# Even heads squared and summed by ScalarE in four accumulating operations, odd heads summed by VectorE

## The reference

```python
h = _layernorm(x, axis=-1) * (1 + ca) + sa
# in the attention part, on h:
q, k, v = ...                       # projections; q and k are rotated
scores = einsum('bhtd,bhsd->bhts', q, k) * D ** (-0.5) * decay
o = einsum('bhts,bhsv->bhtv', scores, v)
mean, var = o.mean(-1), o.var(-1)   # over the 128 values of one head and token
o = (o - mean) * rsqrt(var + EPS)
o = o * gn_weight + gn_bias
o = o * silu(g)
out = einsum('btc,oc->bto', o, Wo)
```

## Time and profile before

| | |
|---|---|
| runs shown | 746.31 us median of 3 (746.22 to 746.49) |
| the profiled execution | 747.0 us, of which its span on the core is 745.2 us |
| TensorE's granted clock | 0.998 of full speed on average |
| busy over the span | TensorE 98%, its weight loads 86%, GpSimd 82%, VectorE 81%, ScalarE 64% |

### The profile page before, as it was taken

The page is one execution under the profiler, slowest core; times in us unless marked ns, Lnnn a source line. Parts: engine busy times, 40 slices in busy tenths (PEclk is TensorE's granted clock), DMA queues, the critical chain, the costliest instruction groups (busy, mean ns, idle before and its releaser), DMA issues.

```text
span 745.2 us, 29021 instructions
## 1 busy us (share of the span) xinstructions
PE 732.8 (98%) x12119; PEld 643.9 (86%) x12119; DVE 604.6 (81%) x1268; ACT 480.6 (64%) x928; POOL 607.5 (82%) x652
## 2 busy tenths in 40 slices
PE   8999999999999999999999999999999999999997
PEld 7778888888889889888888988888888888988986
DVE  4997688888888888888788888888898788787547
ACT  4666657676665666666676665766666666656665
POOL 5887779889798897988889798888979888687640
PEclk9999999999999999999999999999999999999999
DMA  6610020200202121030211303021030201001101
GB/s 251 194 32 18 15 59 15 60 18 13 83 17 77 27 65 39 10 94 17 69 27 21 87 14 88 10 80 30 11 87 17 73 17 31 17 9 31 25 15 29
DMA packets 59809, 35.15 MB, mean 47 GB/s; under 512 B 36664, under 2 KB 54432, under 8 KB 59680
## 3 DMA queue, kind: packets, MB, share of 16 engines
q1 hardware_dynamic: 58960, 32.51, 16.9%
q10 hardware_dynamic: 720, 0.80, 0.3%
HBM read 20.66 MB, written 4.25 MB: 33 GB/s over the span
## 4 chain that ended last, share of the span: by engine, by line
PE 92%; DVE 3%; POOL 2%; ACT 1%; issue 1%; DMA 1%; SPq 0%; DVEq 0%
PE ring L332 51%; PE outs L332 15%; PE O_E L332 14%; PE ring L347 8%; PE O_O L332 3%; PE ring L397 1%; DMA N<-in_w_qkT 1%; POOL gn_rstd L1466 0%; ACT normed L751 0%; POOL y L1473 0%; ACT y L815 0%; DVE N L1146 0%; DVE A L1119 0%; DVE qT L1080 0%; POOL rot_k L1456 0%
## 5 line engine op out<-in xcount | busy, mean ns | idle before, releaser
L1473 POOL TENSOR_TENSOR y<-y,gate 128x512 f32<-128x512 f32 x120 | 158.8, 1337 | 29.4 <-ACT y L815 29.4
L779 ACT ACTIVATE v<-ring 64x512 f32<-64x512 f32 x128 | 76.2, 595 | 80.7 <-PE ring L332 79.9
L332 PEld LDWEIGHTS outs<-wo_gated,y 128*128 128x128 f32 x992 | 119.8, 192 | 6.7 <-DVE y L1185 0.5
L1456 POOL TENSOR_TENSOR rot_k<-rot_k,sin_k 128x256 f32<-128x256 f32 x128 | 102.6, 822 | 26.9 <-DVE sin_k L1112 25.6
L332 PE MATMUL outs<-wo_gated,y 128*128 128x128 f32 x992 | 121.7, 275 | 0.1
L1466 POOL TENSOR_TENSOR gn_rstd<-gn_var,minus_half 128x8 f32<-128x8 f32 x64 | 105.4, 1646 | 5.0
L787 ACT ACTIVATE kT<-ring 128x512 f32<-128x512 f32 x64 | 38.4, 599 | 100.6 <-PE ring L347 100.6
L1139 DVE TENSOR_REDUCE gn_sum<-N 128x4 f32<-128x512 f32 x118 | 75.3, 679 | 26.4 <-ACT N L803 26.4
L1119 DVE TENSOR_TENSOR A<-ring,consts 128x256 f32<-128x256 f32 x128 | 48.4, 419 | 57.5 <-PE ring L332 57.5
L815 ACT ACTIVATE y<-ring,gn 128x512 f32<-128x512 f32 x126 | 91.0, 777 | 5.2 <-PE ring L347 5.2
L1450 POOL TENSOR_TENSOR qT<-qT,swapped 128x512 f32<-128x512 f32 x60 | 77.1, 1284 | 11.3 <-DVE swapped L1095 10.7
(11 more groups left out here) (198 smaller groups left out, 2119.4 us busy)
## 6 DMA issues: line engine op xcount, KB each, us to landing
k_odd<-rot_k SPq DMA_DIRECT2D x128, 64.0 KB, 2.2
row_of<-written_rows SPq DMA_DIRECT2D x12, 512.0 KB, 4.2
X<-in_x SPq DMA_DIRECT2D x16, 256.0 KB, 4.4
out<-X SPq DMA_DIRECT2D x15, 256.0 KB, 2.4
x_turned<-in_xT SPq DMA_DIRECT2D x12, 256.0 KB, 4.6
key_tables<-in_const SPq DMA_DIRECT2D x7, 256.0 KB, 5.1
rotary_q<-in_const_q SPq DMA_DIRECT2D x2, 512.0 KB, 6.1
gates<-stored_rows SPq DMA_DIRECT2D x8, 128.0 KB, 3.1
```

The source lines that it names most:

```text
L332: return e.matmul(o, lhsT, rhs, start=start, stop=stop, skip_group_check=True)
L779: done = e.activation(v[halves(half), i % 2, 1, :, :], by(PAIRS, bank_of["v", odd, i][halves(1 - half), :]), ACT.Copy)
L1456: done = e.tensor_tensor(turned[:, n, :, :], turned[:, n, :, :], sin[:, n, :, :], op)
L1473: e.tensor_tensor(y[:, n % NY, :], y[:, n % NY, :], gate[:, n % 2, :], ALU.mult).then_inc(sem["y"])
```

## The change

In all chunks the even heads now go the way that the first five went: four operations of ScalarE of 128x128, each with its sum. The odd heads are squared in one operation and summed by VectorE as before. VectorE's sum of the even heads is gone.

```diff
@@ -792,7 +792,7 @@ square(i, odd)
                 at.wait_ge("nT_psum", PAIRS * ((i - NN) // GC + 1))
-                if i < EARLY:
+                if i < EARLY or not odd:
                     at.wait_ge("gn_var", i - 1)
                     for n in range(PAIRS):
                         done = e.activation(N[:, i % NN, odd, n, :], heads_of(i)[odd][:, n, :], ACT.Square, accum_out=gn_sum[:, i % 2, odd, n:n + 1])
@@ -1339,8 +1339,6 @@ the loop of block.vector
                 for i in due(step - 1, 1, NCHUNK, 5):
-                    sum_squares(i, 0)
-                for i in due(step - 1, 1, NCHUNK, 5):
                     sum_squares(i, 1)
                 for i in due(step, 1, NCHUNK, 5):
                     add_state(i)
```

## The result

The changed kernel takes 753.78 us, the median of 4 runs (753.71 to 753.82). The kernel before takes 746.26 us beside it (4 runs, 745.98 to 746.49). The ratio is 1.0101, with a 95% interval from 1.0089 to 1.0112: slower by 7.5 us. The profiled execution of the changed kernel took 753.8 us with a span of 752.0, against 747.0 and 745.2 before; by these two it is 6.8 us. The granted clock is 0.998 in both, so the clock has no part in it.

What follows compares the result with a forecast made beforehand. TensorE, busy 98%, was taken as the bound, paying only for new waits on late additions to S: 5.3 us in 35 chunks plus 0.7 at the end, 6.0 on 747.0, as a median 752.3 us, range 749.0 to 758.0.

Steps and rivals of the forecast that it cites:

- No share decides, TensorE's waits do: TensorE is busy 98%: freed VectorE time buys nothing, added ScalarE work costs nothing by itself; only new TensorE waits count.
- The odd square 0.52 us later, from chunk 4 of the same trace: On ScalarE, four even squares with sums take 1.01 us instead of 0.49 before the odd square, in 59 chunks.
- The additions at t + 2.24: On VectorE, additions to S come 2.24 us after the squares start (t), 0.42 or 0.28 us later than before.
- A late load costs 0.15 us: A TensorE weight load 0.28 us late for S costs the stream about 0.15 us; the load's lead takes the rest.
- 35 chunks, 21 and 14, and none at the places of 28 or behind 6: 35 chunks pay, 21 like chunk 27 and 14 like 29, together 5.3 us; those with enough slack pay nothing.
- GpSimd at no cost, ScalarE's cover: GpSimd's power and the scaled heads cost nothing; ScalarE's waits of 1.35 or 0.83 us for TensorE hide its added work.
- The end, 0.7: In the last two chunks the sums are on the path, so delays count in full: 0.28 and 0.42, together 0.7 us.
- The 0.7 us between the profiled execution and the median: The profiled execution of the kernel before, 747.0 us, stands 0.7 over its median, so 753.0 becomes 752.3 us.
- full stalls: Rival: the loads' lead helps less or late scaled heads reach `attend`; 35 x 0.28 plus 0.7 gives 756.8 us; chance 0.20.
- VectorE was the late one: Rival: VectorE reaches the sums late, so dropping one brings additions forward by up to 0.60 us; 744 to 745.1; chance 0.03.

Runs made afterwards that it cites:

- experiment 4: Kernel before without VectorE's sums of the even heads from chunk 5 on, ScalarE as before, output wrong, for timing only: 746.43 us, ratio 1.0001.
- Experiment 6: Changed kernel with the odd heads also squared and summed on ScalarE in four operations, no VectorE sums behind chunk 4: 749.46 us, ratio 1.0044.
- experiment 5: Changed kernel with a fifth ScalarE square from chunk 5 on, the first even head again into an unread tile, ahead of the four: 763.92 us, ratio 1.025.
- experiment 3: Kernel before with VectorE's additions to S ahead of both sums: 751.61 us, ratio 1.0067.
- experiment 1: Changed kernel with VectorE's two additions to S ahead of its one sum: 748.10 us, ratio 1.0024.
- experiment 2: Changed kernel with halves exchanged: ScalarE squares and sums the odd heads in four operations, VectorE sums the even heads: 745.93 us, ratio 0.9993 to the kernel before.
- experiment 7: Changed kernel with VectorE still summing the even heads as well, into an unread tile, ahead of the odd sum: 758.62 us, ratio 1.0168.

## Why the prediction was right

The forecast was 752.3 us, slower, between 749 and 758; it is 753.78. By the steps:

- **No share decides, TensorE's waits do: held.** Experiments 4 and 6 show it from both sides: 35 us off VectorE are worth nothing alone, and 62 us onto ScalarE cost 3.3 us when the additions are not behind them. VectorE's own busy time fell by 30 us and not by the 35 or more that was forecast: the sums took 34.9 us less, but the 15 `delta` (below) took 4.2 more. By the argument itself that changes nothing.
- **The odd square 0.52 us later, from chunk 4 of the same trace: held** (1.01 us in both). The estimate from the Trainium skill (ScalarE: Activation LUTs, section What ACT_TABLE_LOAD costs), 0.80 us for the four, which would have left the time unchanged, is not what the trace shows. The four pitches are 0.26, 0.25, 0.25 and 0.25 us, each with a read of the accumulator in it of 0.19 to 0.22 us that this page does not price.
- **The additions at t + 2.24: nearly.** They are at 2.27, since the odd square lasts 0.62 us and not 0.59 behind accumulating ones, so the sum starts at 1.66.
- **A late load costs 0.15 us: the term that was mis-sized.** It is 0.18 to 0.20 in nearly all tight chunks. I had worked with one load 0.29 late and a lead of 0.13 to 0.14 (0.28 less 0.15 in rows 10). The load is 0.32 late, of which 0.03 is the point above, and the lead that is made good is 0.12 (0.235 less 0.11). The two make 0.04 us a chunk and 1.4 us over the 35, of the 1.5 us by which the forecast fell short.
- **35 chunks, 21 and 14, and none at the places of 28 or behind 6: held**, and a transpose (L397, 14 waits) pays like a projection. The forecast of some 35 waits was half of the 71 that came, since it had overlooked the load behind the first addition. It has no price of its own: its 0.29 us are part of the 0.32 by which the second load is late.
- **GpSimd at no cost, ScalarE's cover: held, but for one chunk** (no load waits for `N` of L1146 ahead of the last chunks). I had said that VectorE catches up at the next mask; in chunk 55 `sin_k` is late before that, for the 0.14 us above. Experiment 6 shows what the cover was worth.
- **The end, 0.7: held**, 0.77.
- **The 0.7 us between the profiled execution and the median: held.** The gap in chunk 5, which no other trace has, is 0.5 to 0.6 us of it.

Of the rivals, "full stalls" wanted 0.28 lost of 0.28. The lead of 0.12 us refutes it, and experiment 5 shows that it is the lead: past it, each 0.25 us costs 0.25. "VectorE was the late one" fell with experiment 4.

Two things stay open. Of experiment 3's smaller losses the largest, 0.4 us in chunk 16, has a gap of 0.44 us among the loads of `state`; the others were not followed to their waits. And what such a gap comes from (0.54 us in chunk 5 of the kernel before, 0.21 in chunk 52 of experiment 1) no trace shows.

## What to carry to other kernels

When an engine's queue holds an item that others wait for, moving work off that engine can delay the item: ask what the item now waits behind, not how much was taken off. If two engines share a job in two halves, give the engine in whose queue others wait the half that is ready first, and do the other half in the slow form (experiment 2 against the change: 7.9 us for the choice of a bank). In these traces a lateness cost TensorE its size less a lead of 0.12 us, once a step, with one load waiting in it (0.15 for 0.28) or two.

## What the runs showed of the hardware

**The lead of weight loads is 0.12 us here.** Behind a load that came late, the next follows at 0.11 us instead of 0.235, once; with lateness of 0.19, 0.32 and 0.57 us the stream lost 0.06, 0.20 and 0.45.

**VectorE and GpSimd hold each other up on some operations.** `delta` (two inputs and its output in SBUF) takes 0.74 us or 1.76 us on VectorE. In the changed kernel's chunk 26 VectorE starts it 0.09 us ahead of GpSimd's product, and GpSimd's is the long one:

```profile
308.58 0.74 DVE L1164 SCALAR_TENSOR_TENSOR delta<-delta,mu,h2T 128x512 f32<-128x512 f32 x1
...
308.67 1.80 POOL L1471 TENSOR_TENSOR y<-y,gate 128x512 f32<-128x512 f32 x1
```

In experiment 7 GpSimd is 0.06 us ahead, and VectorE's is the long one (the 1.76 above):

```profile
309.69 1.27 POOL L1478 TENSOR_TENSOR y<-y,gate 128x512 f32<-128x512 f32 x1
```

Over its 15 instances (least, median and greatest ns) in the changed kernel and in experiment 7:

```profile
L1164 DVE SCALAR_TENSOR_TENSOR delta<-delta,mu,h2T x15: 742/1042/1792, 129.0 to 735.2; 128x512 f32<-128x512 f32 x15
```

```profile
L1169 DVE SCALAR_TENSOR_TENSOR delta<-delta,mu,h2T x15: 746/1761/1787, 128.9 to 739.9; 128x512 f32<-128x512 f32 x15
```

So a shift of 0.15 us decides which engine loses 0.5 to 1 us, and in experiment 7 that cost five chunks 0.3 us each beyond their 0.1. The Trainium skill (SBUF — State Buffer, section Who interferes with whom) says so: a VectorE instruction with two SBUF inputs and a GpSimd instruction that reads SBUF share a read interface, and whichever starts first keeps the other waiting. The traces agree in both directions. The additions to `S`, with one input in the ring, which is in PSUM, take 1.41 us for the two in chunk 27 before and after; before, a product of GpSimd runs beside the first of them, and it takes 1.30 us, near the 1.27 above.
